# Causal stage of a four-stage layer: turned weights in single PSUM banks, guess and correction in two parts, a new order

## The reference

```
qkv = x @ w_qkv + b_qkv            # 16 heads of 16 features
dot = q . k                        # 512 x 512 per head
den = |q|^2 + |k|^2 - 2 dot + 1e-6
scores = dot * dot / den,  masked above the diagonal
out = softmax(scores) @ v,  then @ w_out + b_out
```

## Time and profile before

| | us |
|---|---|
| median of three runs | 4371.79 |
| lowest and highest | 4367.45, 4373.05 |
| the profiled execution | 4363.23 |
| its span, first to last instruction | 4361.2 |
| PE, DVE, ACT, POOL busy in it | 4070.3, 3157.0, 2469.0, 1763.7 |
| mean granted clock of PE, share of full speed | 0.968 |

### The profile page before, as it was taken

One profiled execution on the slowest core, in us unless ns is written; L12 is line 12 of the kernel. 1 busy time (PEld: TensorE's weight loads), 2 busy tenths in 40 slices (PEclk: granted clock), 3 DMA queues, 4 the chain that ended last, 5 costly groups with the idle time before them and its releaser, 6 DMA issues.

```text
span 4361.2 us, 66411 instructions
## 1 busy us (share of the span) xinstructions
PE 4070.3 (93%) x23504; PEld 2586.4 (59%) x23504; DVE 3157.0 (72%) x7625; ACT 2469.0 (57%) x5353; POOL 1763.7 (40%) x2051
## 2 busy tenths in 40 slices
PE   8999999999999999988888888888999999999997
PEld 4666556666666666655555555555666666666664
DVE  6667677777667667658988889888777676677663
ACT  5556554454454545439887788875544544544441
POOL 2223365555546556420111110014555565565551
PEclk9999999999999999998998889989999999999999
DMA  2000000000010000000000000101000000100000
GB/s 78 11 16 6 25 11 6 3 3 6 23 30 11 13 8 8 26 19 20 23 23 20 20 24 23 37 20 33 4 6 3 3 26 8 35 15 18 13 20 22
DMA packets 63176, 78.38 MB, mean 18 GB/s; under 512 B 15312, under 2 KB 47616, under 8 KB 62848
## 3 DMA queue, kind: packets, MB, share of 16 engines
q1 hardware_dynamic: 62848, 74.14, 5.9%
HBM read 36.39 MB, written 12.58 MB: 11 GB/s over the span
## 4 chain that ended last, share of the span: by engine, by line
PE 70%; DVE 14%; ACT 10%; issue 5%; DMA 0%; SPq 0%; POOL 0%; DVEq 0%; ACTq 0%
PE wide L893 48%; PE o_ps L893 8%; PE wide L896 7%; PE turn_ps L896 5%; ACT prob L1270 3%; DVE w_up L1422 2%; PE turn_ps L893 2%; DVE prob L1436 1%; DVE hid L1430 1%; ACT prob L1287 1%; DVE turned L1368 1%; ACT x L1260 1%; ACT hid L1260 1%; DVE ss L1375 1%; DVE turned L1382 1%
## 5 line engine op out<-in xcount | busy, mean ns | idle before, releaser
L893 PE MATMUL wide<-x,w_up 128*128 128x512 f32 (+3 forms) x2528 | 837.5, 540 | 4.2 <-DVE x L1533 2.2
L893 PE MATMUL wide<-w_in,x_t 128*128 128x512 f32 (+2 forms) x1920 | 801.4, 561 | 4.6 <-ACT x_t L1183 1.3
L1661 POOL TENSOR_SCALAR prob<-prob,st 128x256 f32<-128x256 f32 (+1 forms) x1024 | 554.4, 560 | 577.2 <-DVE st L1460 576.6
L1270 ACT ACTIVATE prob<-prob,st 128x256 f32<-128x256 f32 (+1 forms) x1024 | 479.5, 470 | 166.9 <-DVE st L1447 166.5
L893 PEld LDWEIGHTS wide<-x,w_up 128*128 128x128 f32 (+2 forms) x2528 | 374.9, 192 | 300.4 <-issue 283.3
L893 PEld LDWEIGHTS wide<-w_in,x_t 128*128 128x128 f32 x1920 | 339.3, 191 | 332.4 <-issue 323.0
L893 PE MATMUL o_ps<-pt,v 128*32 128x128 f32 (+2 forms) x5120 | 485.1, 332 | 37.8 <-DVE pt L1486 30.6
L1633 POOL TENSOR_TENSOR rn<-ss,minus_half 128x16 f32<-128x16 f32 x128 | 433.7, 3389 | 126.2 <-DVE ss L1377 121.9
L893 PEld LDWEIGHTS o_ps<-pt,v 128*64 128x64 f32 (+1 forms) x5120 | 308.2, 128 | 219.4 <-issue 89.7
L1447 DVE CUSTOM_DVE_ANT_0 prob<-wide,local_mask 128x256 f32<-128x256 f32 (+1 forms) x1024 | 335.3, 382 | 140.4 <-PE wide L893 140.4
L1625 POOL TENSOR_TENSOR sines<-raw,rot 128x512 f32<-128x512 f32 x256 | 351.5, 1394 | 196.7 <-ACT raw L1190 196.7
(11 more groups left out here) (166 smaller groups left out, 7498.9 us busy)
## 6 DMA issues: line engine op xcount, KB each, us to landing
kept<-resid SPq DMA_DIRECT2D x16, 512.0 KB, 2.6
x<-kept SPq DMA_DIRECT2D x16, 512.0 KB, 3.3
w_up<-hid SPq DMA_DIRECT2D x62, 128.0 KB, 2.2
x<-hid SPq DMA_DIRECT2D x62, 128.0 KB, 2.3
shifted<-resid SPq DMA_DIRECT2D x32, 224.0 KB
w_in<-in_f_wqkv SPq DMA_DIRECT2D x4, 1536.0 KB, 6.5
w_up<-in_f_w SPq DMA_DIRECT2D x4, 1492.0 KB, 6.5
resid<-in_x SPq DMA_DIRECT2D x8, 512.0 KB, 7.9
```

Source lines behind the costliest of these rows:

```text
L893: return eng.matmul(out, lhsT, rhs, start=start, stop=stop, skip_group_check=True)
L1270: last = eng.activation(pr[:, local_span(t)], pr[:, local_span(t)], ACT.Exp, bias=sm[:, t:t + 1], scale=-1.0, accum_out=sm[:, 4 + t:5 + t])
L1661: last = eng.tensor_scalar(pr[:, local_span(t)], pr[:, local_span(t)], sm[:, 8 + t:9 + t], 1.0, ALU.mult, ALU.mult)
```

## The change

Three things change, all in units of stage `b`.

1. `turn_b` no longer lives with `turn_a`. Each half takes one bank: `bank6` first, or a single bank of the double rooms if one is free sooner. Where several are free when PE is, the first in the list is taken. A room is let go when its own half is copied. The same transposes, copies and matmuls run.
2. ACT's `bguess` becomes `bln` (the logarithms) and `bguess` (the exponential), and DVE's `bmul` becomes `binv` (the factor) and `bmul` (products and maxima). They are parts of their own for the scheduler, with costs of their own, so that other parts may stand between them. The instructions are the same.
3. The table `DUE` for `b` has other numbers and more entries, and with it the order of every engine is another from unit 22 (the feed-forward units that run into the causal stage) to the start of unit 32. Before and after that the orders are the same.

```diff
         "ACT": "... bk_c bq_c bnum bguess exp pt_a out olog gelu",      # before
         "ACT": "... bk_c bq_c bnum bln bguess exp pt_a out olog gelu",  # after; DVE's list gains binv
-B_COST = {"bnum": (0.1, 0.21), "bguess": (0.45, 0.45), "bclose": (0.1, 0.277), "bmul": (0.45, 0.525),
+B_COST = {"bnum": (0.1, 0.21), "bln": (0.32, 0.24), "bguess": (0.1, 0.21), "binv": (0.1, 0.277), "bclose": (0.1, 0.277), "bmul": (0.35, 0.25),
...
-    ("b", "res"): -0.004, ("b", "row"): -0.121, ("b", "xt"): -0.042, ("b", "bmul"): 0.075, ("b", "bdot"): -0.135,
+    ("b", "res"): -0.004, ("b", "row"): -0.192, ("b", "bmul"): 0.075, ("b", "bdot"): -0.135, ("b", "olog"): 0.03,
...
-            put("bguess", k, at + .5 / steps, final("bdot", k), final("brow", 3), ("bmul", *three), *ffn)
+            put("bln", k, at + .5 / steps, final("bdot", k), final("brow", 3), ("bmul", *three), *ffn)
+            put("bguess", k, at + .5 / steps, final("bln", k))
             put("bclose", k, at + 1 / steps, final("bguess", k))
-            put("bmul", k, at + 1.5 / steps, final("bclose", k), final("bnum", k), *scaled)
+            put("binv", k, at + 1.5 / steps, final("bclose", k))
+            put("bmul", k, at + 1.5 / steps, final("binv", k), final("bnum", k), *scaled)
...
     kind, u, i = part
-    if kind == "turn_b" and stage_of(u) == "b":
-        return ("turn_a", u, i)
     return (kind, u, 0) if kind in ("proj", "down") else part
...
-    if kind in NARROW and not (kind == "turn_a" and st == "b"):
+    if st == "b" and kind in ("turn_a", "turn_b"):
+        return [single] + [(f"bank{k}", (k,)) for k in reversed(range(BANKS - 1))]
+    if kind in NARROW:
         return [single]
...
+            if at is not None and stage_of(u) == "b":
+                at = max(at, free_at["PE"])
...
-            elif kind == "turn_a" and stage_of(u) == "b":
+            elif kind == "turn_a":
                 pe.wait_ge(S[first_copy(u, i)], nth(first_copy(u, i), u, i))
-                pe.wait_ge(S["pt_b"], nth("pt_b", u, i))
...
-                        to, at = turned_to(i, k, block), k * b_width(i) + block * P
+                        to, at = turned_to(i, k, block) % 512, k * b_width(i) + block * P
...
-                    act.wait_ge(S["bln"], o)
+                elif kind == "bguess":
+                    inv = close_home(u, i)[1]
+                    exp_tables()
+                    act.wait_ge(S["bln"], nth("bln", u, i))
                     eng.activation(inv, inv, ACT.Exp, scale=-1.0).then_inc(S["bguess"], 1)
...
+                elif kind == "binv":
+                    den, inv = close_home(u, i)
+                    dve.wait_ge(S["bclose"], nth("bclose", u, i))
+                    eng.scalar_tensor_tensor(out=inv, in0=den, scalar=2.0, in1=inv, op0=ALU.subtract, op1=ALU.mult
+                                             ).then_inc(S["binv"], 1)
                 elif kind == "bmul":
...
-                    dve.wait_ge(S["binv"], o)
-                    dve.wait_ge(S["bnum"], o)
+                    dve.wait_ge(S["binv"], nth("binv", u, i))
+                    dve.wait_ge(S["bnum"], nth("bnum", u, i))
```

More of the change, by code:

```diff
@@ L156 @@
         "PE": "fold_q fold_o xt qk vv spread aq lat bqkv bk bq score bden bdot turn_a turn_b mix sel fan proj xt2 up_g up_h down",
-        "ACT": "fold_q_c xt_c raw v_c q_c aq_c av_c bsq bk_c bq_c bnum bguess exp pt_a out olog gelu",
-        "DVE": "fold_o_c bn_h nrm_h cos ss join k_c ak_c row bss bclose bmul low inv pt_b pt_c osum out_b res bn_f bn_f2 nrm_f xt2_c gate hid res2",
+        "ACT": "fold_q_c xt_c raw v_c q_c aq_c av_c bsq bk_c bq_c bnum bln bguess exp pt_a out olog gelu",
+        "DVE": "fold_o_c bn_h nrm_h cos ss join k_c ak_c row bss bclose binv bmul low inv pt_b pt_c osum out_b res bn_f bn_f2 nrm_f xt2_c gate hid res2",
         "POOL": "rstd_h sin rn brow neg bias_b wt rstd_f bias back rot pad_out pad_down pad_v",
@@ L453 @@
 READERS = {"xt": ["xt_c"], "qk": ["raw"], "vv": ["v_c"], "spread": ["q_c", "k_c"], "aq": ["aq_c"], "lat": ["ak_c", "av_c"],
-           "fold_q": ["fold_q_c"], "fold_o": ["fold_o_c"], "bqkv": ["row"], "bk": ["bk_c"], "bq": ["bq_c"], "bden": ["bguess", "bclose"],
+           "fold_q": ["fold_q_c"], "fold_o": ["fold_o_c"], "bqkv": ["row"], "bk": ["bk_c"], "bq": ["bq_c"], "bden": ["bln", "bguess", "bclose"],
            "bdot": ["bnum"], "score": ["low", "exp"], "turn_a": ["pt_a", "pt_c"], "turn_b": ["pt_b"], "sel": ["olog", "osum"], "fan": ["out_b"], "xt2": ["xt2_c"],
@@ L487, in readers_of @@
     last = [(r, u, 0 if kind in ("proj", "down") else i) for r in READERS[kind]]
-    if kind == "turn_a" and stage_of(u) == "b":
-        last.append(("pt_b", u, i))
     if kind == "score" and stage_of(u) == "f":
@@ L1251, in scalar_program @@
                                    ).then_inc(S["bnum"], 1)
-                elif kind == "bguess":
+                elif kind == "bln":
                     inv, w, ps = close_home(u, i)[1], b_width(i), wide[PLACE["bden", u, i]]
@@ L1477, in vector_program @@
                         dve.wait_ge(S["const"], 16 * 3)
-                        ps, met, n = wide[PLACE["turn_b", u, i]], P * B_OWN[i % 3], P * len(B_TURNS[i % 3][1])
-                        last = eng.tensor_tensor(blocks(pt[:, 512:512 + met]), blocks(ps[:, 512:512 + met]),
+                        ps, met, n = buffers[PLACE["turn_b", u, i]], P * B_OWN[i % 3], P * len(B_TURNS[i % 3][1])
+                        last = eng.tensor_tensor(blocks(pt[:, 512:512 + met]), blocks(ps[:, 0:met]),
                                                  causal_keep[:, :].unsqueeze(1).to_broadcast([P, met // P, P]), ALU.mult)
                         if n > met:
-                            last = eng.tensor_copy(pt[:, 512 + met:512 + n], ps[:, 512 + met:512 + n])
+                            last = eng.tensor_copy(pt[:, 512 + met:512 + n], ps[:, met:n])
                         last.then_inc(S["pt_b"], 1)
```

10 lines of the change are left out of this document (2 added, 8 removed), and 16 rows, old and new, of the table DUE.

## The result

Four runs of the changed kernel took 4306.59 to 4313.97 us, median 4309.61; four of the kernel before 4363.86 to 4373.05 us, median 4369.62. The ratio is 0.986, with a 95% interval of 0.9845 to 0.9875: 60 us faster. The forecast was 28 us. The direction was right and the time lies inside the range, next to the rival "everything goes" (4308), which had 0.15.

What follows compares the result with a forecast made beforehand. It took the causal stage's body as bound by DVE and ACT together, most loss in the change-over. Terms -10 - 14 + 3 - 7 = -28 us gave 4335 against the profiled execution, 4344 as median; range 4302 to 4388 us.

Steps and rivals of the forecast that it cites:

- everything goes: Rival: all long half-speed stretches vanish (-22), change-over gives 30 us, body 12: -64, 4308 us; chance 0.15.
- The body: Middle of each causal-stage sequence, bound by DVE and ACT: 10 us gained, at most 27 from idle time.
- The split: Guess and correction queued in two parts, so fewer waits on an engine's own result: 7 us of DVE.
- the rooms: Turned weights in single PSUM banks shorten PE's waits for copies; bound 0 to 27 us in the body.
- The change-over: Between causal sequences: new order saves PE 3.1 us each, 2 let through, 7 times: 14 us.
- the clock: Less PE idle time at change-overs spares one long half-speed stretch: 7.4 us; ends 22 gained or 37 lost.
- The three long stretches: Half-speed PE around the projection in three of five change-overs; 7.4 us each, one expected to go.
- The place that the term named: PE's 3.33 us wait at the change-over's first `row`, to end 1.96 us earlier with statistics moved.
- The same seventh bank: Both halves share it in 26 of 192 steps, adding waits: 3 us lost, 0 to 21 possible.
- right: Causal-stage signs: periods 122 to 128 us, copy waits under 70, first `row` gap under 1.5, body DVE above 96%.
- No change: Rival: body waits only move and PE's own work sets the change-over: -5 us, 4367; chance 0.15.
- Slower through the clock: Rival: PE idles on the seventh bank, half-speed stretch in every sequence's change-over: +27, 4399 us; chance 0.15.

Runs made afterwards that it cites:

- both_body: Changed kernel, but in steps 5 to 17 PE again waits for both copies of a step before reusing either half's room; 4332.3 us, 0.993 of the kernel before.
- dve_closed: Changed kernel with each correction factor on DVE put back right ahead of its product; 4373.1 us, 1.0008 of the kernel before.
- warm_before: Kernel before with six useless matmuls into the idle seventh bank ahead of `bk` at each change-over; 4353.6 us, 0.9976 of the kernel before.
- act_closed: Changed kernel with each logarithm on ACT put back right ahead of its exponential; 4348.4 us, 0.9953 of the kernel before.
- warm_after: Changed kernel with five useless matmuls ahead of step 0's `turn_b` in six change-overs; 4334.4 us, 0.9935 of the kernel before.
- banks_only: Kernel before with single banks for the halves and the new due table, guess and correction undivided; 4405.7 us, 1.0088 of the kernel before.

## Why the prediction was wrong

**The body, -10 us forecast, -25.1 measured: this is the step that failed.** The term took the gain out of the body's idle time alone ("at most the body's idle", 27 us) and held DVE's 57 us of work in it fixed. At clock 1.00 the body lost 4.0 us, and only 1.0 of them is idle time of DVE. Another 1.1 us is the overlap of parted pairs (108 of the 186 lie in steps 8 to 20, 13.5 a body at 0.08), which shows in busy time and not in the idle column; the remaining 2 us are work put off into the change-over, for which the forecast had no term. Three sizes were off with it. The split was priced from the idle column, "10.5 us of DVE for 165 steps", 0.03 us of a pair instead of 0.11, and 29 of its 82 parted factors had been parted before: 7 us, where the 186 pairs take 20. The pairs on ACT, 13 us, were put at nothing. And the rooms were left 3 of the 10 us, "a little over a third of the 27": undoing them costs a body 1.8 us at full clock (`both_body`), 13 us in seven. DVE's busy time of a whole sequence bears the price of a pair out: 57.05 + 58.37 = 115.4 us before, 53.96 + 59.43 = 113.4 after, with the same instructions, and 186/8 = 23 pairs at 0.08 are 1.9.

What is shown for the body is thus each part's price in the changed order: rooms 1.8 us, ACT's split 1.3, and 1.0 for the part of DVE's split that `dve_closed` puts back. That these add up to 4.1 is chance, since that run puts back 70 of 186 pairs and none of the three brings the moved work back. Seven times 4.0 are 28; 25.1 came, since two of the bodies after read 0.94.

**The change-over and the clock, -14 and -7 forecast, -23.1 measured together.** The sum was near, the shares were not. The kernel before gives lengths at three clocks in the earlier trace rows's sequences: 64.8 us at 0.95, 66.6 at 0.90, 73.1 at 0.79. Read between these, the change-overs of sequences 2 to 6 after would take 336.3 us at their own clocks; they took 329.4, and before 350.8. By this estimate, which rests on three lengths alone, the clock gave 14.5 us and the order, with the split, 6.9; the first and the last change-over, 1.7 us shorter together, are not in it. Half of the change in the time at half speed, (184 - 149)/2 = 17.6 us, is the most that the clock can have given in the whole stage, an estimate that lets half the clock double the time of everything that ran at it. So the clock's term was about half of its size and the order's about twice. The three long stretches, of which one was to go, all went, and came back in part as shorter ones. `warm_before` lies on the same scale (65.9 by it at 0.92, 66.1 measured). The place that the term named changed as forecast: the first `row` no longer holds PE up for 3.33 us, and PE's waits for `row` are 1.6 us in all, against 17.7. But the longest wait there is still 2.29 us, now for a copy. DVE works without a gap from the factor below to that copy, and this factor takes 2.37 us where others of its shape take 0.95: it stands beside an addition on POOL, also 2.37 us, and ends 0.8 us behind it. This is so in four change-overs after and in four before (2.36 us instead of 1.22); no run moved the addition, so its part is not shown.

```profile
2421.85 2.37 POOL L1594 TENSOR_TENSOR resid<-resid,bias_row 128x1024 f32<-128x1024 f32 x1 [2.03 <-DVE turned L1337]
2422.66 2.37 DVE L1434 SCALAR_TENSOR_TENSOR x<-w_up,x 128x768 f32<-128x768 f32 x1
...
2427.43 0.80 PE L896 MATMUL wide<-hid 18*128 18x256 f32 x2 [2.29 <-DVE pt L1489]
```

**The same seventh bank, +3 forecast, nothing seen.** PE's waits in that bank, those of the 26 steps among them, are 17.1 us. No run took them away, so what they cost in the end is open.

**Outside the middle, nothing forecast, -5.5 measured** at the stage's two ends: 2.3 us ahead of the first body, 8.7 in the body of the eighth sequence (80.6 to 71.9 us), of which what follows it loses 5.5 again. No run took this apart. With the terms: -28, -15.1 for the body, -2.1 for change-over and clock, -3 and -5.5 make -53.7.

**The signs.** Those named for "right" came: periods of 120 to 123 us, 44 us of waits of the scores for copies, no wait of more than 0.5 us for a `row`, DVE at 96.2% of the body (53.96 of 56.09). They told the direction; none of them could tell -28 from -54.

**The rivals.** "No change" fell: the waits did not only change their names. "Everything goes" came true in time, but by luck of its sizes: 12 for the body, 30 for the order and 22 for the clock, so it was right on the long stretches and wrong on where the rest lies. "Slower through the clock" did not happen, though kernels close to the changed one show what it describes: in `act_closed` and `warm_after` a half-speed stretch of 17 us comes into sequences that had none. Those kernels lose 41 and 33 us by the ratios; by the halves of their added time at half speed the clock can account for at most 28 and 18 of that.

The page "TensorE: Matmul & The Clock Gate" of the Trainium skill, section "A second HAM failure mode: psum-queue depth-cycling", ties repeated drops of the clock to small idle gaps of a PE that cycles through PSUM banks. The forecast's reading of it, more single banks and so more drops, fits `banks_only` (273 us at half speed, 184 before) and not the changed kernel (149). What decides is not shown: over five sequences, from step 8 of the second to step 8 of the seventh, PE idles 110 us before, 75 after and 100 in `banks_only`, with some 120, 79 and 181 us at half speed, so idle time alone does not order them either.

What stays open: why a given sequence falls to half speed and its neighbour with the same order doesn't (`both_body` has bodies at 1.00 and at 0.84), and why the long stretch comes in `warm_after`. No run has the split alone with the old table, or the order of the changed kernel with neither edit, so how the gain divides among order, banks and split is not settled beyond the prices above. The costs of undoing one part, 22 to 65 us, add up to far more than the gain: in most of them there are 1 to 2 us of a body at full clock, of which the pairs explain about half, and the clock on top, which was not reckoned ahead. None of these kernels beat the changed one.

## What to carry to other kernels

Price the parting of two dependent instructions from the starts in the timeline, a parted pair against a pair back to back, times the pairs; here the idle column showed a quarter of it. Count only the pairs that the change parts newly. When two cuts of a trace are compared, count the instructions in them before calling the difference a gain: here half of the body's was work that had moved behind the cut. Where an engine's clock changes between runs, compare stretches at equal clock first and add the clock as a term with both signs: here an edit that costs a body 1.0 us at full clock moved the whole by 65. An order made for one set of edits is part of them: the table alone brought nothing, and the two edits without it cost 19 us.

## What the runs showed of the hardware that was not expected

- Matmuls that compute nothing made a kernel faster: 42 of them in the seven change-overs, 10 us (`warm_before`), though the first and the last change-over became longer; 30 of them at another place made the changed kernel 33 us slower (`warm_after`).
- PE can fall to half speed while it is busy without a gap: 2447 to 2455 us after, busy 8.00 of 8.00 at 0.57, after full speed from 2434 to 2447 at 12.68 of 13. Among what it ran in the 8 us before were the four fans, matmuls with 4 rows; that they are the cause is not shown.
- An instruction that waits for nothing starts ahead of the recorded end of the one before it, 0.08 us on DVE and 0.10 to 0.12 us on ACT; so the recorded busy time of an engine falls when the order parts dependent pairs, with no instruction less (DVE 15.7 us, ACT 12.0).
- A factor on DVE took 2.37 us instead of 0.95 (before 2.36 instead of 1.22) wherever one addition on POOL ran beside it, in four change-overs of either kernel.
